# Packing the expert tables of a routed feed-forward layer into one word per entry

## The chip, the cores and the metric

The kernel runs on one core of a Trainium2 chip. The metric is the time of one execution on the device in microseconds. The time before is 2512.99 us, the median of three runs (2507.62 to 2515.87 us).

## The reference

One layer: linear attention with a residual, then a mixture of experts with a residual. The part that matters here is the second, over 4096 tokens of 512 numbers, with 32 experts, 8 of them for each token.

```python
E, K, H, F = 32, 8, 512, 192
scores = softmax(x @ wg.T)
weights, idx = top_k(scores, K)
weights = weights / sum(weights, axis=-1, keepdims=True)
order = argsort(idx.reshape(-1))                  # rows sorted by expert
xs = x[t_s]
g = ragged_dot(xs, w1, group_sizes)
u = ragged_dot(xs, v1, group_sizes)
ys = ragged_dot(silu(g) * u, w2, group_sizes)
out = zeros(T, H).at[t_s].add(ys * w_s[:, None])
...
x = x + layernorm(attention(layernorm(x)))
x = x + layernorm(moe(layernorm(x)))
```

How many rows an expert gets is known only at run time.

## The kernel before

The kernel has an attention part (to about 1165 us), a short stage that builds tables (to about 1211 us), the expert stage (to about 2440 us) and a final layer norm with the residual.

During the attention part every token's row is written eight times into a buffer in memory that is sorted by expert, in pages of 256 rows. In the table stage VectorE turns the page counts into tables in row 0 of the tile `bq`, as 32-bit integers:

- `table`, one column per expert: row 0 holds the expert's number of tiles `n`, row 1 the number of its `first` tile, row 2 the place of its padding rows (SyncE alone reads it), row 3 the value of the semaphore `s_D` (the count of `down` products) from which the expert before the last has left its weight slot. This block starts at L620 and ends with the signal `s_tabd` at L651. ScalarE, VectorE and SyncE wait for it.
- `at_tile`, one column per tile: row 0 holds the offset of the tile's weights in the tile `WB` (one of four slots, `WSET` = 4608 columns each), row 1 the first tile of its expert (GpSimd reads it), row 2 the place of its rows in memory (SyncE reads it). Column `g + 2` belongs to tile `g`. This block (L679 to L683) follows two small matrix products and ends with the signal `s_tiles`, for which SyncE, TensorE and GpSimd wait. Between the two blocks a list of pages is brought from memory (L356), and TensorE sums comparisons with it (L425).

In the expert stage a tile is 128 sorted rows of one expert. There are 276 tiles. Each number is split into a high part (float32r) and the rest, so that every product is made as three. For a tile TensorE does, in this order, `rows_t` of the tile after (four transposes, L437), `up` (12 matmuls of 384 columns, L446 to L448), `act_t` of the tile before (two transposes, L456) and `down` of the tile two before (five matmuls of 512 columns, L463 to L467). The loop over tiles is a hardware loop with four tiles per turn (L479). At the start of each tile TensorE's sequencer reads two words with `slot_at` (L470): the weight offset of the tile two before, for `down`, and that of the tile itself, for `up`.

ScalarE does for each tile `silu` (L513), the high part of the transposed activations (L518), the copy of `down`'s result to one of four buffers in `Y` (L524) and the high part of the transposed rows (L508). VectorE does the gate (L712, L715), the low part of the activations (L722), the tile's index for the add (L727) and the low part of the rows (L702, L704). GpSimd adds the result to the sum in memory with an indirect DMA (L1449). Waits are for semaphores, whose value is mostly computed from the tile's number in a register.

ScalarE and VectorE go by experts: `each_expert` (L291) reads `n` (L299) and `first` (L300) for an expert, then calls `convert`, then runs a hardware loop over the expert's `n` tiles (L565 on ScalarE, L754 on VectorE). `convert` splits the weights of the expert two ahead into one of the four slots, in six pieces: ScalarE writes the high part (L503), VectorE the low one (L601). ScalarE's `convert` reads a third word (L545), waits until `s_D` has reached it (L546) and issues, between its pieces, the transfers of the weights of the expert three ahead (L319 to L324). VectorE's `convert` reads nothing more. For the last two experts there is nothing to convert.

Of the kernel before, what the change touches and what calls it, by code (L numbers as in the profile page):

```python
# [7 lines left out]
EXPERTS, TOP_K, FFN = 32, 8, 192  # L8
P = 128
TOKENS = BATCH * SEQ  # L10
# [19 lines left out]
WSET = 2 * W13 + 3 * HID  # L30
WSETS = 4
# [13 lines left out]
def layer(nc, x_in, wkv_in, bq_in, bkv_in, wq_in, wo_in, wg_in, w13_in, w2_in, out):  # L45
# [9 lines left out]
    with ctx:  # L55
# [104 lines left out]
        tn = bq[:, 0:ES].rearrange("p (i n) -> p i n", i=4)  # L160
        step = bq[:, ES:ES + 2 * EXPERTS].rearrange("p (i n) -> p i n", i=2)
        table = bq[0:1, 2 * ES:2 * ES + 4 * EXPERTS].bitcast(i32).rearrange("p (i n) -> p i n", i=4)
        pair_n = bq[0:1, 3 * ES:3 * ES + 1].bitcast(i32)
        listed = bq[:, 3 * ES + 2:3 * ES + 2 + 2 * TILES // 4].rearrange("p (k j) -> p k j", j=2)
        at_listed = bq[:, 3 * ES + 32:3 * ES + 32 + TILES // 4]
# [128 lines left out]
        def each_expert(eng, convert, body):  # L294

            eng.wait_ge(s_tabd, 1)

            def one(e, q):
                n = eng.value_load(table[0:1, 0, bass.ds(e, 1)], min_val=1, max_val=TOKENS // P + 1)  # L299
                first = eng.value_load(table[0:1, 1, bass.ds(e, 1)], min_val=0, max_val=MAX_TILES)  # L300
                convert(e, q)
                body(e, q, first, n)
                return first + n

            with eng.Fori(0, EXPERTS // WSETS - 1) as r:
                for q in range(WSETS):
                    one(r * WSETS + q, q)
            for e in range(EXPERTS - WSETS, EXPERTS):
                total = one(e, e % WSETS)
            return total  # L310
# [102 lines left out]
        def moe_pe(pe):  # L413

            pe.sem_inc(s_T, RSLOTS)
            pe.sem_inc(s_U, 1)
            pe.sem_inc(s_H, 1)
            pe.sem_inc(s_D, 1)

            steps = TILES // 4  # L420
            pe.wait_ge(s_pld, 64)
            for k in range(steps + 1):
                pe.wait_ge(s_pcmp, k + 1)
                pages_of = listed[:, k, 1:2] if k < steps else col[:, 3:4]
                nc.tensor.matmul(bank[5][0:1, 0:MAX_TILES], pages_of, same[k % COMPARES], start=k == 0, stop=k == steps).then_inc(s_pmm, 1)  # L425

            pe.wait_ge(s_cmp, 1)
            for i in range(2):
                last = nc.tensor.matmul(bank[6 + i][0:1, 0:MAX_TILES], col[:, i:i + 1], iota_g[:, :], start=True, stop=True)
            last.then_inc(s_tmm, 1)  # L430

            def rows_t(g, i, p):
                s = i % 2
                pe.wait_ge(s_ld[i], 16 * p + 16)
                pe.wait_ge(s_exl, g)
                for k in range(KC):
                    last = nc.tensor.transpose(et[s][:, k * P:(k + 1) * P], xr[:, i, k * P:(k + 1) * P], ident[:, :])  # L437
                last.then_inc(s_T, 1)

            def up(g, s, off):  # L440
                pe.wait_ge(s_exl, g + 2)
                pe.wait_ge(s_h, g + 1)
                for k in range(KC):
                    wh = WB[:, bass.ds(off + k * UP, UP)]
                    wl = WB[:, bass.ds(off + (W13 + k * UP), UP)]
                    nc.tensor.matmul(eu[s][:, 0:UP], XL[:, s, k, :], wh, start=k == 0, stop=False)  # L446
                    nc.tensor.matmul(eu[s][:, 0:UP], XH[:, s, k, :], wh, start=False, stop=False)  # L447
                    last = nc.tensor.matmul(eu[s][:, 0:UP], XH[:, s, k, :], wl, start=False, stop=k == KC - 1)  # L448
                last.then_inc(s_U, 1)

            def act_t(g, s):

                pe.wait_ge(s_h, g + 3)
                pe.wait_ge(s_hl, g + 2)
                for c in range(2):
                    last = nc.tensor.transpose(eh[s][:, c * P:(c + 1) * P], hx[:, s, c * P:(c + 1) * P], ident[:, :])  # L456
                last.then_inc(s_H, 1)

            def down(g, s, off):
                pe.wait_ge(s_hl, g + 4)  # L460
                pe.wait_ge(s_y, g + 3)
                w2h, w2l, w2x = [WB[:, bass.ds(off + o, HID)] for o in (W2H, W2L, W2X)]
                nc.tensor.matmul(ed[s], SL[:, s, 0, :], w2h, start=True, stop=False)  # L463
                nc.tensor.matmul(ed[s], SH[:, s, 0, :], w2h, start=False, stop=False)  # L464
                nc.tensor.matmul(ed[s], SH[:, s, 0, :], w2l, start=False, stop=False)  # L465
                nc.tensor.matmul(ed[s], SL[:, s, 1, :], w2x, start=False, stop=False)  # L466
                nc.tensor.matmul(ed[s], SH[:, s, 1, :], w2x, start=False, stop=True).then_inc(s_D, 1)  # L467

            def slot_at(i):
                return pe.value_load(at_tile[0:1, 0, bass.ds(i, 1)], min_val=0, max_val=(WSETS - 1) * WSET)  # L470

            pe.wait_ge(s_ld[0], 16)
            for k in range(KC):
                last = nc.tensor.transpose(et[0][:, k * P:(k + 1) * P], xr[:, 0, k * P:(k + 1) * P], ident[:, :])
            last.then_inc(s_T, 1)
            pe.wait_ge(s_tiles, 1)
            pairs = pe.value_load(pair_n[0:1, 0:1], min_val=TOKENS * TOP_K // P // 2, max_val=PAGES // 2)

            with pe.Fori(0, pairs >> 1) as p:  # L479
                for i in range(RSLOTS):  # L480
                    g, s = RSLOTS * p + i, i % 2
                    before, now = slot_at(g), slot_at(g + 2)
                    rows_t(g + 1, (i + 1) % RSLOTS, p + (i + 1) // RSLOTS)
                    up(g, s, now)
                    act_t(g - 1, 1 - s)
                    down(g - 2, s, before)

            total = 2 * pairs
            rows_t(total + 1, 1, pairs >> 1)
            act_t(total - 1, 1)  # L490
            down(total - 2, 0, slot_at(total))
            down(total - 1, 1, slot_at(total + 1))

        def moe_act(act):

# [42 lines left out]
            act.wait_ge(s_T, RSLOTS + 2)  # L538
            nc.scalar.activation(XHF[:, HID:2 * HID], PS[:, ET + HID:ET + 2 * HID], ACT.Copy).then_inc(s_exh, 1)

            def convert(e, q):
                if isinstance(e, int) and e + 2 >= EXPERTS:
                    return
                load = not (isinstance(e, int) and e + 3 >= EXPERTS)
                before = act.value_load(table[0:1, 3, bass.ds(e, 1)], min_val=1, max_val=MAX_TILES + 3)  # L545
                act.wait_ge(s_D, before)  # L546
                stand(act)
                if load:
                    act.wait_ge(s_elo, e + 2)
                    stand(act)  # L550
                for piece in range(len(PIECES)):
                    weights_high(e + 2, (q + 2) % WSETS, q % 2, piece)
                    if load and piece < 4:
                        load_weights(act, e + 3, (q + 1) % 2, piece)
# [31 lines left out]
        def moe_dve(dve):  # L586
# [23 lines left out]
            def done(inst):  # L610
                tab[0] += 1
                inst.then_inc(s_tab, 1)

            def settled():
                dve.wait_ge(s_tab, tab[0])
# [20 lines left out]
            done(nc.vector.scalar_tensor_tensor(odd[:, 1:2], odd[:, 0:1], float(YSLOTS), total, ALU.mult, ALU.subtract))  # L636
            done(nc.vector.tensor_copy(step[:, 1, 1:EXPERTS], tn[:, 2, 0:EXPERTS - 1]))
            done(nc.vector.memset(step[:, 1, 0:1], 0.0))
            done(nc.vector.memset(step[:, 0, :], float(WSET)))
            settled()  # L640
            done(nc.vector.tensor_tensor(tn[:, 3, :], tn[:, 3, :], tn[:, 2, :], ALU.subtract))
            done(nc.vector.memset(step[:, 0, :].rearrange("p (r q) -> p r q", q=WSETS)[:, :, 0:1], float((1 - WSETS) * WSET)))
            done(nc.vector.tensor_scalar(odd[:, 2:3], odd[:, 0:1], float(YSLOTS // 2), None, ALU.mult))
            settled()
            done(nc.vector.memset(step[:, 0, 0:1], 0.0))
            done(nc.vector.tensor_tensor(tn[:, 2, EXPERTS - 1:EXPERTS], tn[:, 2, EXPERTS - 1:EXPERTS], odd[:, 1:2], ALU.add))
            settled()
            nc.vector.tensor_copy(table[:, 0:2, :], tn[0:1, 2:4, :])
            nc.vector.memset(table[:, 3, 0:1], 1)
            nc.vector.tensor_scalar(table[:, 3, 1:EXPERTS], tn[0:1, 3, 0:EXPERTS - 1], 3.0, None, ALU.add)  # L650
            nc.vector.tensor_copy(pair_n[:, :], odd[0:1, 2:3]).then_inc(s_tabd, 1)  # L651
            for i, (which, src) in enumerate(((ident[:, 0:EXPERTS], step[:, 0, :]), (ident[:, 0:EXPERTS], step[:, 1, :]), (fours, tn[:, 3, :]),
                                              (ident[:, 0:EXPERTS], iota_e[:, :]))):
# [22 lines left out]
            dve.wait_ge(s_pcmp, steps + 1)  # L676
            nc.vector.tensor_scalar(iota_g[:, :], iota_g[:, :], col[:, 2:3], None, ALU.is_ge).then_inc(s_cmp, 1)
            dve.wait_ge(s_tmm, 1)
            nc.vector.memset(at_tile[:, :, 0:2], 0)  # L679
            for i in range(2):  # L680
                nc.vector.tensor_copy(at_tile[:, i, 2:2 + MAX_TILES], bank[6 + i][0:1, 0:MAX_TILES])
            dve.wait_ge(s_pmm, steps + 1)
            nc.vector.tensor_scalar(at_tile[:, 2, 2:2 + MAX_TILES], bank[5][0:1, 0:MAX_TILES], float(PAGE), None, ALU.mult).then_inc(s_tiles, 1)  # L683

# [51 lines left out]
                nc.vector.tensor_tensor(XLF[:, half], PS[:, ET + i * HID:ET + (i + 1) * HID], XHF[:, half].bitcast(f32),  # L736
                                        ALU.subtract).then_inc(s_exl, 1)

            def convert(e, q):
                if isinstance(e, int) and e + 2 >= EXPERTS:  # L740
                    return
                for piece in range(len(PIECES)):
                    weights_low(e + 2, (q + 2) % WSETS, q % 2, piece)
# [836 lines left out]
```

## Time and profile before

| | |
|---|---|
| median of 3 runs | 2512.99 us |
| profiled execution | 2513.74 us |
| its span, first to last instruction | 2512.0 us |
| busy in the span: TensorE, VectorE, ScalarE, GpSimd | 90%, 59%, 49%, 38% |
| mean granted clock of TensorE | 0.955 of full |
| memory traffic over the span | 142 GB/s |

The table is from the profile's page and the list of runs. Busy time of an engine is time in which one of its instructions ran; register instructions and table loads of a sequencer are not counted in it. They have rows of their own, in which the engine's name ends in q (ACTq, DVEq, PEldq). A matmul's end is modelled, so two that follow each other overlap in the rows, and the distance of their starts is what TensorE takes for one. "issue" as the reason of a wait means that no signal of another engine is seen that ended it.

### The profile page before, as it was taken

Reading aid. Unit: us, or ns where it says so; the run is one execution under the profiler, and the core shown is the slowest. Engines: PE = TensorE matmul, PEld = TensorE weight load, DVE = VectorE, ACT = ScalarE, POOL = GpSimd, SP = SyncE. Lnnn points to the kernel's source line nnn. Section 1 sums busy time; section 2 is a strip of 40 time slices with the busy share of each in tenths; the row PEclk is TensorE's granted clock in tenths of the full one; section 3 lists DMA queues with packets and bytes.
Section 4 is the critical chain, followed back from the end, with each engine's and each line's share of the span. In section 5 each row is a group of like instructions: output and inputs, shape, how many; then the busy total and the mean of one; then the engine's idle time right before and its main releaser. Section 6 shows DMA issues by size and latency. Waiting matters only on the chain.

```text
span 2512.0 us, 63405 instructions
## 1 busy us (share of the span) xinstructions
PE 2250.3 (90%) x11850; PEld 1921.8 (77%) x11851; DVE 1488.6 (59%) x4833; ACT 1235.1 (49%) x2643; POOL 952.3 (38%) x1128
## 2 busy tenths in 40 slices
PE   7999899999989999991798999989999889989980
PEld 5887588888858888881597888868889778978970
DVE  4455567777767777773545555555554555455446
ACT  3344466656656665651344444454444444444433
POOL 1212025555535555556133333323333233323332
PEclk9999999999999999995899999999999999999995
DMA  3234103333342333325798888877777787777767
GB/s 118 89 116 121 59 26 115 120 114 128 122 134 103 123 119 114 128 102 196 200 204 179 179 190 185 170 178 164 151 150 140 169 162 156 140 168 142 139 111 288
DMA packets 165278, 358.64 MB, mean 143 GB/s; under 512 B 21216, under 2 KB 21216, under 8 KB 165088
## 3 DMA queue, kind: packets, MB, share of 16 engines
q0 software_dynamic: 60512, 144.74, 29.3%
q1 hardware_dynamic: 91264, 173.89, 23.3%
q10 hardware_dynamic: 13440, 39.33, 4.7%
q8 instruction: 22, 0.36, 0.1%
q14 instruction: 40, 0.33, 0.0%
HBM read 178.21 MB, written 179.66 MB: 142 GB/s over the span
## 4 chain that ended last, share of the span: by engine, by line
PE 37%; issue 5%; ACTq 4%; DMA 2%; ACT 2%; DVE 1%; DVEq 1%; POOL 1%; SPq 0%; POOLq 0%
PE bank L446 6%; PE bank L448 6%; PE bank L447 6%; PE bank L437 5%; PE bank L463 3%; PE bank L456 2%; PE bank L467 2%; PE bank L465 2%; PE bank L466 2%; PE bank L464 2%; ACTq L324 1%; ACT WB L503 1%; DVEq L712 1%; ACT BIG L582 1%; DMA moe_sum<-Y,aidx 1%
## 5 line engine op out<-in xcount | busy, mean ns | idle before, releaser
L1449 POOL DMA_INDIRECT moe_sum<-Y,aidx x276 | 428.6, 1553 | 835.5 <-issue 480.9
L929 PE MATMUL bank<-WB,XH 128*128 128x512 f32 x1536 | 477.1, 392 | 0.0
L446 PE MATMUL bank<-WB,XL 128*128 x1104 | 401.3, 363 | 0.0
L448 PE MATMUL bank<-WB,XH 128*128 x1104 | 375.7, 340 | 0.0
L447 PE MATMUL bank<-WB,XH 128*128 x1104 | 374.5, 339 | 0.0
L929 PEld LDWEIGHTS bank<-WB,XH 128*128 128x128 f32 x1536 | 290.4, 189 | 58.1 <-issue 0.5
L929 PE MATMUL bank<-WB,XL 128*128 128x512 f32 x768 | 315.5, 411 | 10.4 <-DVE XL L1236 10.4
L929 PE MATMUL bank<-WB,SH 128*128 128x512 f32 x1024 | 317.2, 391 | 0.0
L712 DVE SCALAR_TENSOR_TENSOR BIG<-BIG,bank x276 | 95.9, 347 | 363.1 <-ACT BIG L513 211.2
L1515 POOL DMA_INDIRECT sorted_rows<-BIG,pos x256 | 265.6, 1038 | 95.3 <-issue 95.3
L513 ACT ACTIVATE BIG<-bank x276 | 91.4, 331 | 354.5 <-PE bank L448 338.8
L524 ACT ACTIVATE Y<-bank x278 | 166.5, 599 | 180.7 <-PE bank L467 144.8
L1199 ACT ACTIVATE BIG<-BIG,rec 128x128 f32<-128x128 f32 x512 | 163.6, 390 | 181.2 <-DVE rec L1308 170.1
L929 PEld LDWEIGHTS bank<-WB,SH 128*128 128x128 f32 x1024 | 192.7, 188 | 37.6
L929 PE MATMUL bank<-WB,SL 128*128 128x512 f32 x512 | 211.0, 412 | 2.8 <-DVE WB L1298 2.8
L446 PEld LDWEIGHTS bank<-WB,XL 128*128 128x128 f32 x1104 | 213.1, 193 | 0.0
L447 PEld LDWEIGHTS bank<-WB,XH 128*128 128x128 f32 x1104 | 213.0, 193 | 0.0
L448 PEld LDWEIGHTS bank<-WB,XH 128*128 128x128 f32 x1104 | 210.8, 191 | 0.0
L1457 POOL TENSOR_SCALAR ve<-mv 128x1 f32<-128x1 f32 x128 | 47.0, 367 | 424.8 <-DVE mv L1227 302.1
L704 DVE TENSOR_TENSOR XL<-bank,XH x276 | 190.9, 692 | 18.0 <-ACT XH L508 3.8
L437 PEld LDWEIGHTS bank<-ident,BIG 128*128 128x128 f32 x1108 | 136.0, 145 | 76.2 <-issue 50.5
L437 PE MATMUL bank<-ident,BIG 128*128 128x128 f32 x1108 | 177.2, 284 | 16.4 <-issue 14.2
(211 smaller groups left out, 4265.2 us busy)
## 6 DMA issues: line engine op xcount, KB each, us to landing
BIG<-sorted_rows SPq DMA_DIRECT2D x278, 274.0 KB
Y<-x_in SPq DMA_DIRECT2D x64, 256.0 KB, 2.8
RAW<-w_in ACTq DMA_DIRECT2D x15, 768.0 KB
LATE<-w_in ACTq DMA_DIRECT2D x15, 768.0 KB
sorted_rows<-BIG SPq DMA_DIRECT2D x33, 274.0 KB, 12.3
moe_sum<-LATE SPq DMA_DIRECT2D x34, 256.0 KB, 3.0
LATE<-x_in SPq DMA_DIRECT2D x32, 256.0 KB
RAW<-wo_in SPq DMA_DIRECT2D x16, 512.0 KB, 3.5
```

The source lines that it names most:

```text
L437: last = nc.tensor.transpose(et[s][:, k * P:(k + 1) * P], xr[:, i, k * P:(k + 1) * P], ident[:, :])
L446: nc.tensor.matmul(eu[s][:, 0:UP], XL[:, s, k, :], wh, start=k == 0, stop=False)
L447: nc.tensor.matmul(eu[s][:, 0:UP], XH[:, s, k, :], wh, start=False, stop=False)
L448: last = nc.tensor.matmul(eu[s][:, 0:UP], XH[:, s, k, :], wl, start=False, stop=k == KC - 1)
L513: nc.scalar.activation(BIG[:, at(SG, parity, FFN, FFN)], PS[:, at(EU, parity, HID, FFN)], ACT.Silu).then_inc(s_sg, 1)
L524: nc.scalar.activation(YF[:, bass.ds(((g + YSLOTS) & (YSLOTS - 1)) * HID, HID)], PS[:, at(ED, parity, HID, HID)], ACT.Copy).then_inc(s_y, 1)
L704: nc.vector.tensor_tensor(XLF[:, at(0, parity, HID, HID)], PS[:, at(ET, parity, HID, HID)], XHF[:, at(0, parity, HID, HID)].bitcast(f32), ...
L712: nc.vector.scalar_tensor_tensor(BIG[:, at(HX, parity, 2 * P, P)], BIG[:, at(SG, parity, FFN, P)], w, PS[:, at(EU + FFN, parity, HID, P)], ...
L929: last = nc.tensor.matmul(ps, w, m, start=start and i == 0, stop=stop and i == len(terms) - 1)
L1199: last = nc.scalar.activation(sqn[:, c % 2, h * P:(h + 1) * P], e[:, c % 2, h * P:(h + 1) * P], ACT.Copy, scale=rec[:, c % 2, h:h + 1])
L1449: nc.gpsimd.indirect_dma_start(acc_dram[:, :], bass.IndirectOffsetOnAxis(aidx[:, s:s + 1], 0), rows, None, compute_op=ALU.add).then_inc(s_ ...
L1515: nc.gpsimd.indirect_dma_start(sorted_dram[:, :], bass.IndirectOffsetOnAxis(pos[:, s, k:k + 1], 0), srow[:, s, :], None).then_inc(s_sc[s], 16)
```

## The change

The tables are packed and the readers unpack them in registers.

- Each column of `table` row 0 becomes one word, `before * 32768 + n * 512 + first`. It is built in float32 from two partial sums and written as an integer. ScalarE and VectorE read it once per expert, in place of three and two words.
- The slots of the tiles are no longer summed up as offsets of `WB` but as numbers of experts (the step from one expert to the next is 1), and column `g` of `at_tile` row 0 becomes the expert of tile `g` plus 64 times the expert of tile `g - 2`. TensorE reads it once per tile, takes each slot with a mask of two bits and multiplies it by `WSET`.
- VectorE's two table blocks get the instructions for this. GpSimd's and SyncE's reads stay.

```diff
+        words = bq[0:1, 7 * ES - EXPERTS:7 * ES]
...
             def one(e, q):
-                n = eng.value_load(table[0:1, 0, bass.ds(e, 1)], min_val=1, max_val=TOKENS // P + 1)
-                first = eng.value_load(table[0:1, 1, bass.ds(e, 1)], min_val=0, max_val=MAX_TILES)
-                convert(e, q)
+                word = eng.value_load(table[0:1, 0, bass.ds(e, 1)], min_val=512 + 32768, max_val=512 * 32768 - 1)
+                first, n, before = word & 511, (word >> 9) & 63, word >> 15
+                convert(e, q, before)
...
-            def slot_at(i):
-                return pe.value_load(at_tile[0:1, 0, bass.ds(i, 1)], min_val=0, max_val=(WSETS - 1) * WSET)
+            def slots_at(i):
+
+                word = pe.value_load(at_tile[0:1, 0, bass.ds(i, 1)], min_val=0, max_val=64 * EXPERTS - 1)
+                return (word & (WSETS - 1)) * WSET, ((word >> 6) & (WSETS - 1)) * WSET
...
-                    before, now = slot_at(g), slot_at(g + 2)
+                    now, before = slots_at(g)
...
-            def convert(e, q):
+            def convert(e, q, before):
...
-                before = act.value_load(table[0:1, 3, bass.ds(e, 1)], min_val=1, max_val=MAX_TILES + 3)
                 act.wait_ge(s_D, before)
...
-            done(nc.vector.memset(step[:, 0, :], float(WSET)))
+            done(nc.vector.memset(step[:, 0, :], 1.0))
...
-            done(nc.vector.memset(step[:, 0, :].rearrange("p (r q) -> p r q", q=WSETS)[:, :, 0:1], float((1 - WSETS) * WSET)))
...
-            nc.vector.tensor_copy(table[:, 0:2, :], tn[0:1, 2:4, :])
-            nc.vector.memset(table[:, 3, 0:1], 1)
-            nc.vector.tensor_scalar(table[:, 3, 1:EXPERTS], tn[0:1, 3, 0:EXPERTS - 1], 3.0, None, ALU.add)
+            done(nc.vector.scalar_tensor_tensor(tn[0:1, 0, :], tn[0:1, 2, :], 512.0, tn[0:1, 3, :], ALU.mult, ALU.add))
+            done(nc.vector.memset(words[:, 0:1], 32768.0))
+            done(nc.vector.tensor_scalar(words[:, 1:EXPERTS], tn[0:1, 3, 0:EXPERTS - 1], 3.0, 32768.0, ALU.add, ALU.mult))
+            settled()
+            nc.vector.tensor_tensor(table[:, 0, :], words, tn[0:1, 0, :], ALU.add)
...
-            nc.vector.memset(at_tile[:, :, 0:2], 0)
-            for i in range(2):
-                nc.vector.tensor_copy(at_tile[:, i, 2:2 + MAX_TILES], bank[6 + i][0:1, 0:MAX_TILES])
+            nc.vector.memset(at_tile[:, 1:3, 0:2], 0)
+            nc.vector.tensor_copy(at_tile[:, 1, 2:2 + MAX_TILES], bank[7][0:1, 0:MAX_TILES])
+            done(nc.vector.tensor_copy(iota_g[0:1, :], bank[6][0:1, 0:MAX_TILES]))
+            settled()
+            nc.vector.tensor_copy(at_tile[:, 0, 0:2], iota_g[0:1, 0:2])
+            nc.vector.scalar_tensor_tensor(at_tile[:, 0, 2:MAX_TILES], iota_g[0:1, 0:MAX_TILES - 2], 64.0, iota_g[0:1, 2:MAX_TILES], ALU.mult, ALU.add)
+            nc.vector.tensor_scalar(at_tile[:, 0, MAX_TILES:MAX_TILES + 2], iota_g[0:1, MAX_TILES - 2:MAX_TILES], 64.0, None, ALU.mult)
```

## Rows read from the trace of the kernel before

**Rows 1.** Stretches: length, busy us of each engine, granted clock, DMA share, GB/s.
```profile
1213.00:2440.00 1227.00, 1139.63 (x6359) 1016.08 (x6359) 646.15 (x1842) 573.61 (x1286) 425.22 (x274) 0.97 0.80 165
```

**Rows 2.** Timeline of TensorE: start, length, line, operation, idle before.
```profile
1705.50 0.61 PE L437 MATMUL bank<-ident,BIG 128*128 128x128 f32 x4
...
1709.20 0.40 PE L467 MATMUL bank<-WB,SH 128*128 x1
1709.43 0.60 PE L437 MATMUL bank<-ident,BIG 128*128 128x128 f32 x4
...
1719.76 0.39 PE L467 MATMUL bank<-WB,SH 128*128 x1
1720.61 0.63 PE L437 MATMUL bank<-ident,BIG 128*128 128x128 f32 x4 [0.47 <-issue]
```

**Rows 3.** Waits, 1213 to 2440: who, for what, us in total, times, longest.
```profile
POOL moe_sum L1449 <- issue: 480.9, 189, 45.4
...
PE bank L456 <- DVE BIG L715: 69.4, 31, 3.4
...
ACT Y L524 <- POOLq L815: 16.9, 21, 1.5
...
PE bank L437 <- issue: 14.2, 32, 1.0
...
ACT WB L503 <- PE bank L467: 9.3, 3, 3.5
...
ACT WB L503 <- DMA RAW<-w_in: 6.5, 2, 3.4
ACT WB L503 <- DMA LATE<-w_in: 6.3, 2, 3.3
```

**Rows 4.** The chain of waits, 1710 to 1722: start, length, what.
```profile
1711.45 0.05 ACTq L300
...
1712.06 0.05 ACTq L545
...
1712.70 0.07 issue
...
1716.54 0.04 DVEq L754
...
1717.08 0.05 DVEq L712
1717.17 0.04 DVEq L712
...
1717.58 0.12 DVE BIG L712
```

**Rows 5.** Lines L545, L549, L300: ns min/median/max, first and last start.
```profile
L545 ACTq TENSOR_LOAD <-bq x30: 273/275/897, 1217.0 to 2275.2; - x30
...
L549 ACTq ALU_OP  x7: 35/35/42, 1217.7 to 2089.8; - x7
...
L300 DVEq TENSOR_LOAD <-bq x32: 300/306/777, 1217.2 to 2345.0; - x32
```

**Rows 6.** Line L470, whole and 1718.9 to 1720.5; L463, 1700 to 1704.
```profile
L470 PEldq TENSOR_LOAD <-bq x554: 295/301/1036, 1212.1 to 2438.9; - x185
...
L470 PEldq TENSOR_LOAD <-bq x2: 299/301/303, 1719.0 to 1719.8; - x2
...
L463 PEldq FUSED_REGOPS  x1: 46/46/46, 1702.9 to 1702.9; - x1
```

**Rows 7.** Timeline of VectorE.
```profile
1702.45 0.42 DVE L722 TENSOR_TENSOR SL<-bank,SH  x1
```

**Rows 8.** The chain of waits, 1180 to 1212.
```profile
1184.50 12.64 DMA bq<-page_list
```

**Rows 9.** Timeline of VectorE in the second table block.
```profile
1205.73 0.44 DVE L681 CAST bq<-bank 1x290 int32<-1x290 f32 x1 [1.32 <-issue]
...
1206.46 0.44 DVE L683 TENSOR_SCALAR bq<-bank 1x290 int32<-1x290 f32 x1
```

More of the change, by code:

```diff
@@ L490, in moe_pe @@
             act_t(total - 1, 1)
-            down(total - 2, 0, slot_at(total))
-            down(total - 1, 1, slot_at(total + 1))
+            down(total - 2, 0, slots_at(total)[1])
+            down(total - 1, 1, slots_at(total + 1)[1])
         def moe_act(act):
@@ L737, in moe_dve, with convert @@
                                         ALU.subtract).then_inc(s_exl, 1)
-            def convert(e, q):
+            def convert(e, q, before):
                 if isinstance(e, int) and e + 2 >= EXPERTS:
```

## Prediction

> **What bounds the kernel now.** I read three views in this order. The view by stretches for the expert stage, 1213 to 2440 us [rows 1], shows TensorE busy for 1139.6 of 1227 us, against 646 for VectorE and 574 for ScalarE: TensorE is the bound, and what is to be won is the rest. 276 tiles pass in the stage (554 loads of a slot [rows 6], two a tile and two at the end). The timeline of TensorE [rows 2] gives the pace of an undisturbed tile: its first transpose (L437) starts at 1705.50 and that of the next at 1709.43, so 3.93 us. 276 x 3.93 = 1085 us of 1227, so some 142 us are lost in the stage. The list of waits [rows 3] says on what. The largest is L456, the transpose of the activations, waiting for VectorE's gate (L715): 69.4 us in 31 waits, 2.2 us each. There are 30 experts whose turn carries a weight conversion (the third load of ScalarE, x30 [rows 5]), so this is one stall per expert. The second is L437 waiting for "issue", 14.2 us in 32 waits: TensorE's own sequencer comes too late with the next tile. The modelled end of L467 hides part of each: L467 to L437 is 0.23 us where nothing is missing (1709.20 to 1709.43) and 0.85 after a stall (1719.76 to 1720.61), of which the view calls 0.47 idle [rows 2]. So 0.16 a time belongs on top: 14.2 + 32 x 0.16 = 19 us. Third, the granted clock is 0.97 over the stage [rows 1]; with levels of 1 and 0.5 that is 6% of the stage, 74 us, at 1.2 GHz, which costs at most 37 us. 69 + 19 + 37 is 125 of the 142; the rest is spread over short waits and the stage's two ends.
>
> **ScalarE: two of three loads go.** The chain of waits through one turn of expert [rows 4] shows the stall's making. After the last XH of the old expert ScalarE's sequencer reads three table entries before it can start the conversion: the second runs from 1711.45 to 1712.06, the third from 1712.06 to 1712.70. Those two are removed: 0.61 + 0.64 = 1.25 us. In their place come shifts and masks on the word. On ScalarE only the shift for the count of `s_D` stands ahead of the conversion; such a register instruction took 0.035 us [rows 5], with what lies around it 0.07. The masks for `first` and `n` are needed only by the tile loop, which is issued while the last conversion piece still runs. So the conversion starts 1.18 us earlier.
>
> **VectorE: one of two loads goes.** Its load takes 0.306 us [rows 5] and with its address and its check about 0.75. It stands beside ScalarE's loads, since VectorE cannot convert before ScalarE's first piece. VectorE's chain matters at the other end: from L754, the entry to the tile loop, at 1716.54, to the gate L712 at 1717.58 is 1.04 us of register instructions, 0.09 from one to the next (1717.08 to 1717.17) [rows 4]. If the two masks and the shift for `first` and `n` are worked out there, they add 0 to 0.27 us; I take 0.2. The turn then gains 1.18 - 0.2, about 1.0 us. That is less than the stall of 2.2, so it comes off fully.
>
> It does not come off at every turn. Seven times ScalarE's conversion waited, with the loads done, for something else: 3 times for TensorE's L467 (9.3 us) and 4 times for a weight transfer (6.5 and 6.3 us) [rows 3]. These are experts of few tiles, where the transfer was issued by the turn before. I count nothing for them and 0.15 us each for the masks, 1 us lost. So 23 x 1.0 - 1 = 22 us. Bounds: 0.7 to 1.25 us a turn, that is 15 to 29.
>
> A rule of the Trainium skill would price the load otherwise: "DMA: Bandwidth & Descriptors", section "Latency and other measured facts", puts the floor of a `tensor_load` at about 600 ns. By that two loads less would be 1.9 us a turn, 1.6 after the masks, and the term 36 us; the trace has 0.3 us for the load itself [rows 5, 6], and its number is used.
>
> **TensorE: one of two loads a tile goes.** After a stall the two loads start at 1719.0 and 1719.8 [rows 6], with address and check 0.75 us each, and L437 follows. Without a stall they matter less, but do matter: down's wait is for a register's value, so the sequencer stands at it until VectorE's L722 ends at 1702.87 [rows 7], and issues L463's first register instruction at 1702.9 [rows 6]; down, the loop's branch and two loads then take it to 1705.3, when the array has just run dry. One load less is 0.75. The new mask, shift, mask and two multiplications are at most five register instructions of 0.09 (0.45), at least nothing where they fold into those that are there; I take 0.3, so 0.45 net. 32 waits x 0.45 = 14 us, and 3 for those too short to be listed: 17. Bounds: 5 (all five instructions in the way, and the short waits stay) and 24 (nearly all of the lost time).
>
> **The clock.** At a turn the array now stands for 2.2 us, then 0.6 again; afterwards 1.2 and about 0.1. Whether the grant falls less often the trace of before can't show. It is bounded by 0 and 37 us; the idle time halves, but the grant fell at some turns only, so I take a quarter, 9. A worse phase could also cost some: -5 at the low end.
>
> **What is added.** In the first table block VectorE has one dependent step more, some 0.3 us, covered by the page list's transfer, which is the chain itself from 1184.5 to 1197.1 [rows 8] while the block runs beside it. Without that cover it would cost those 0.3 us. In the second block three conversions of 1 x 290 follow each other from 1205.73 to 1206.90 [rows 9], and SyncE, TensorE and GpSimd wait for the last. Added behind them: the wait for a result, two operations of a few elements (0.1 each) and one of 1 x 290, 0.3 to 0.44: +0.6 us, all on the path. No DMA, queue or wait on a semaphore between engines is added.
>
> **What comes nearer.** The adds into `moe_sum` run on GpSimd's queue. ScalarE waited 21 times, 16.9 us, until one freed a buffer [rows 3]. With turns shorter this grows in the stretches with short experts. GpSimd itself waited 480.9 us for work [rows 3], so the adds can't bound the stage. I take 3 us.
>
> **Sum.** 22 + 17 + 9 - 0.6 - 3 = 44 us. The profiled execution took 2513.74 us (span 2512.0), 0.75 above the median of the runs; 2513.7 - 44 = 2469.
>
> **Rivals.**
> (A) TensorE's part is nothing: the masks and multiplications cost what the load cost, and the clock stays. For it: the sequencer runs ahead of the array for most of a tile. Against it: the 32 waits. Then 22 - 4 = 18 us: 2495. The Trainium skill speaks for (A): "Advanced Engine Details and Errata", section "Engine Queue Depths", gives TensorE a queue of 64, which would hide any load behind more than a tile's matmuls. By rows 6 and 7 the queue doesn't fill, because the wait for a register's value holds the sequencer itself.
> (B) The clock gives back most: 30 of 37 us instead of 9: 2449.
> (C) The turn is ended by something else than the loads, as it was 7 times: weights or adds come no earlier, and ScalarE waits at the conversion instead. Only TensorE's 17 less 3 are left, or with (A) nothing: 2500 to 2513, middle 2506. Against it: in the other turns the conversion started 0.2 us after the last load.
> (D) Slower: the masks are not kept but worked out again at each use. TensorE's `up` and `down` form an address in 11 register instructions a tile; with two more each of 0.09, the sequencer needs 2 us more a tile. It has 3.93 us for a tile and reaches the next transposes just in time now; less the 0.75 saved it would be late by 0.3 us or more from the point where the added instructions exceed the load removed. 276 x 0.3 = 83 us, less the turns' 22: 2575. Against it: a slot read before is used in the same 11 instructions with no repeated work.
>
> **How the numbers follow.** Forecast 0.52, (A) 0.20, (B) 0.13, (C) 0.10, (D) 0.05. A measurement of this kernel can tell 0.3%, 7.5 us, from no change. Faster by more: forecast, (A), (B) and half of (C), 0.90; within: half of (C), 0.05; slower: (D), 0.05. The forecast's own range, from the terms' bounds, is 2448 to 2490. The range takes in (A) and nearly all of (B) and leaves out (D) and most of (C): 2444 to 2498.
>
> **What would show it.** Right: L456's wait for L715 falls from 69 to about 45 us with as many waits; L437's wait for "issue" falls below 3; ScalarE shows one load a turn with the conversion's first piece some 1.2 us nearer to the last XH; the granted clock of the stage is 0.975 or more; `s_tiles`' last conversion ends 0.6 us later than now after the last table matmul. Wrong: as many masks in TensorE's register instructions as matmuls (D); waits of L503 on transfers in many more than 4 turns (C); L437's "issue" unchanged (A). The forecast fails as a whole if the stall at a turn isn't shortened by what ScalarE's loads gave up.

## The result, and the profile after

The kernel after takes 2478.39 us (median of 4 runs, 2474.85 to 2481.75) against 2513.86 for the kernel before beside it (2507.62 to 2515.87): ratio 0.9863, 95% interval 0.9841 to 0.9885. A later set of runs gave 2481.98 against 2515.14, ratio 0.9862 (0.9841 to 0.9884). By these the change saves 33 to 35 us, where 44 were forecast. The profiled execution of after took 2481.75 us (span 2479.9), 32 us less than the profiled one of before.

The list of waits of the kernel after over the expert stage, 1213 to 2440 us, as in [rows 3]: who waits, for what, us in total, times, longest. L457 is the old L456, L438 the old L437, L464 the old L463, L506 the old L503, L722 the old L715.
```profile
PE bank L457 <- DVE BIG L722: 63.5, 31, 5.7
...
ACT WB L506 <- DMA LATE<-w_in: 21.3, 5, 5.9
...
ACT Y L527 <- POOLq L822: 11.3, 15, 2.2
...
ACT WB L506 <- DMA RAW<-w_in: 9.2, 2, 5.5
...
PE bank L464 <- issue: 7.6, 26, 1.1
...
PE bank L438 <- issue: 1.1, 4, 0.3
```
A second profiled execution of this kernel (2479.12 us) has for the first of these rows:
```profile
PE bank L457 <- DVE BIG L722: 57.1, 30, 6.0
```
Against [rows 3] the reader is to see four things. The next tile's transposes are no longer late: 14.2 us in 32 waits have become 1.1 in 4. A wait that is nearly all new, 7.6 us in 26 (0.9 in 1 before), stands one step earlier, ahead of down's first matmul. The stall at an expert's turn fell by only 6 us, from 69.4 to 63.5, in the second execution by 12, and its longest grew from 3.4 to 5.7 and 6.0. And ScalarE's conversion waits 30.5 us in 7 places for a weight transfer (27.3 in 7 in the second execution), where it was 12.8 us in 4.

From the start of the first transposes inside the loop over tiles to the start of those behind it, in TensorE's timeline, the 276 tiles take 1190.1 us, against 1222.4 before (1184.9 in the second execution). So the 32 us between the profiled executions all lie in this stage.

An ordinary turn in TensorE's timeline (start, length, line, operation, idle before), first of the kernel before, then the same turn in the kernel after:
```profile
1718.24 0.44 PE L456 MATMUL bank<-ident,BIG 128*128 128x128 f32 x2 [2.19 <-DVE BIG L715]
```
```profile
1699.80 0.44 PE L457 MATMUL bank<-ident,BIG 128*128 128x128 f32 x2 [1.52 <-DVE BIG L722]
1700.49 0.49 PE L464 MATMUL bank<-WB,SL 128*128 x1 [0.26 <-issue]
...
1701.52 0.40 PE L468 MATMUL bank<-WB,SH 128*128 x1
1701.76 0.61 PE L438 MATMUL bank<-ident,BIG 128*128 128x128 f32 x4
```
The stall is 0.67 shorter. L468 to L438 is 0.24 us, the undisturbed distance, where it was 0.85 with 0.47 called idle [rows 2]. In its place 0.26 us of idle stand ahead of L464.

At the same turn ScalarE's timeline shows the conversion after its loads:
```profile
1712.92 0.53 ACT L503 ACTIVATE WB<-RAW 128x384 fp32r<-128x384 f32 x1 [1.97 <-issue]
```
```profile
1694.18 0.53 ACT L506 ACTIVATE WB<-RAW 128x384 fp32r<-128x384 f32 x1 [1.01 <-issue]
```
Counted over that timeline, the time from the end of the last XH of an expert to the start of the conversion has a median of 2.06 us before and 0.92 after (0.78 in the second execution), over 29 turns.

Two turns that follow each other closely, in the kernel before and in the kernel after (TensorE's timeline, then of after also ScalarE's and the chain):
```profile
1348.08 0.44 PE L456 MATMUL bank<-ident,BIG 128*128 128x128 f32 x2 [2.51 <-DVE BIG L715]
...
1357.29 0.44 PE L456 MATMUL bank<-ident,BIG 128*128 128x128 f32 x2 [3.21 <-DVE BIG L715]
```
```profile
1343.40 0.44 PE L457 MATMUL bank<-ident,BIG 128*128 128x128 f32 x2 [0.93 <-DVE BIG L722]
...
1353.02 0.69 PE L457 MATMUL bank<-ident,BIG 128*128 128x128 f32 x2 [4.91 <-DVE BIG L722]
```
```profile
1347.16 0.53 ACT L506 ACTIVATE WB<-LATE 128x384 fp32r<-128x384 f32 x1 [4.21 <-DMA LATE<-w_in]
```
```profile
1339.67 7.47 DMA LATE<-w_in
1347.16 0.06 ACT WB L506
```
The first stall fell from 2.51 to 0.93, the second rose from 3.21 to 4.91: 5.72 us together before, 5.84 after. The transfer for the second turn is issued by the first turn's conversions, and the second conversion starts as it lands. The distance of the two stalls' ends was 9.21 us and is 9.62. At this pair, what is saved at the first turn is waited for at the second.

Of the table part, the chain of waits of the kernel after, 1150 to 1222, still holds the transfer of the page list, as in [rows 8], so the longer first block is covered by it:
```profile
1184.00 13.74 DMA bq<-page_list
```
VectorE's timeline of the second block answers to [rows 9]:
```profile
1206.13 0.44 DVE L683 CAST bq<-bank 1x290 int32<-1x290 f32 x1 [1.32 <-issue]
...
1206.50 0.44 DVE L684 COPY bq<-bank 1x290 f32<-1x290 f32 x1
1206.97 0.16 DVE L686 CAST bq<-bq 1x2 int32<-1x2 f32 x1
1207.04 0.44 DVE L687 SCALAR_TENSOR_TENSOR bq<-bq 1x288 int32<-1x288 f32 x1
...
1207.48 0.44 DVE L690 TENSOR_SCALAR bq<-bank 1x290 int32<-1x290 f32 x1
```
From the start of the block's first conversion to the end of its last it is 1.79 us (1206.13 to 1207.92), where it was 1.17 (1205.73 to 1206.90): the added work is 0.6 us.

### The profile page after: what moved, and what is told of

Its sections match the earlier page's. It is cut to its first block, busy times and chain, and to the rows that moved or that the text cites. A ratio compares the mean times of both kernels' runs of the same rounds, so it can differ in the third digit from the quotient of the medians.

```text
span 2479.9 us, 64600 instructions
## 1 busy us (share of the span) xinstructions
PE 2232.1 (90%) x11850; PEld 1921.0 (77%) x11851; DVE 1485.7 (60%) x4836; ACT 1233.3 (50%) x2643; POOL 951.7 (38%) x1128
## 4 chain that ended last, share of the span: by engine, by line
PE 38%; issue 5%; DMA 4%; ACTq 3%; ACT 2%; DVE 1%; DVEq 1%; SPq 0%; POOL 0%; POOLq 0%
PE bank L447 6%; PE bank L449 6%; PE bank L448 6%; PE bank L438 4%; PE bank L464 3%; PE bank L457 2%; PE bank L468 2%; PE bank L466 2%; PE bank L465 2%; PE bank L467 2%; DMA LATE<-w_in 2%; ACTq L325 1%; ACT WB L506 1%; DMA moe_sum<-Y,aidx 1%; ACT BIG L584 1%
## 5 line engine op out<-in xcount | busy, mean ns | idle before, releaser
L438 PEld LDWEIGHTS bank<-ident,BIG 128*128 128x128 f32 x1108 | 141.0, 144 | 44.3 <-issue 6.0
L438 PE MATMUL bank<-ident,BIG 128*128 128x128 f32 x1108 | 171.4, 278 | 2.8 <-DMA BIG<-sorted_rows 1.7
```

## The experiments

All are timed in five rounds against the kernel before, except the two with smaller transfers (three).

**1. Which part gives what.** The experts' word alone, on the kernel before:
```
+                word = eng.value_load(table[0:1, 0, bass.ds(e, 1)], ...)
+                first, n, before = word & 511, (word >> 9) & 63, word >> 15
```


> The experts' word alone: ScalarE and VectorE read one word, TensorE still reads two. Theory (the saved loads come off at the isolated turns, but where the next turn waits for its weight transfer the gain ends in that wait): ScalarE's loads fall from 64 to about 22 us in the 30 turns, the wait between loads and conversion rises by 12 us or more, L456's stall falls by 10 to 20 us, the time by 12 to 20 us. Rival (the two parts don't interfere and the experts' part is the 22 us that were forecast, TensorE's the rest): 21 to 23 us faster. Rival (the experts' part gives nothing, all of the measured 35 us is TensorE's): within 5 us of before.

And TensorE's word alone:
```
+                word = pe.value_load(at_tile[0:1, 0, bass.ds(i, 1)], ...)
+                return (word & (WSETS - 1)) * WSET, ((word >> 6) & (WSETS - 1)) * WSET
...
-                    before, now = slot_at(g), slot_at(g + 2)
+                    now, before = slots_at(g)
```


> TensorE's word alone: one read a tile, ScalarE and VectorE as before. Theory: the wait of L437 for issue goes from 14.2 us to about 1, but in pairs of turns tied by a weight transfer what it gives is taken back by the wait for the transfer, and the masks ahead of down add 0.2 us a turn; 14 to 20 us faster. The sum of this and the experts' part alone is below or near the whole, 35 us. Rival (TensorE's part is the whole gain): 33 us or more faster. Rival (the masks cost what the load cost): within 5 us.

Measured: 2491.75 us, ratio 0.990 (0.9885 to 0.9915), and 2508.51, ratio 0.9967 (0.9953 to 0.9981), both against 2515.81. That is 24 us for the experts' word (above the 12 to 20 of the theory, close to the rival's 21 to 23) and 7 for TensorE's; together 31, and the whole change 33 to 35, so by their times the two nearly add up. TensorE's part alone is smaller than the term of 17, and below the 14 to 20 us that were expected of it. The waits of the kernel with TensorE's word alone, 1213 to 2410:
```profile
PE bank L457 <- DVE BIG L721: 73.2, 30, 4.4
...
PEld bank L438 <- issue: 6.2, 27, 0.5
PE bank L464 <- issue: 5.4, 21, 0.3
...
PE bank L438 <- issue: 0.2, 1, 0.2
```
L438's 14.2 us went, as forecast. But 5.4 came back at L464, and the turns' stall rose by 4, from 69.2 in the same stretch of the kernel before.

The times alone don't say where each part was won. For that, take the distance from the start of each matmul to the start of the next in TensorE's timeline over the 276 tiles, and sum up by how much each is above the median for its place. What is left, 1053 to 1057 us, is 276 tiles of medians. "Other" is all distances that are at none of the three places; it holds the time at the lower clock and the short waits, and can't be split further by these rows.

| kernel | ahead of `act_t` | ahead of the next transposes | ahead of `down` | other | 276 tiles, us |
|---|---|---|---|---|---|
| before | 74.5 | 25.5 | 8.8 | 60.5 | 1222.4 |
| experts' word alone | 59.3 | 29.4 | 8.4 | 49.8 | 1200.2 |
| TensorE's word alone | 78.2 | 4.6 | 14.3 | 63.6 | 1215.3 |
| after | 68.1 | 3.6 | 14.6 | 49.1 | 1190.1 |
| after, second execution | 61.6 | 4.1 | 14.3 | 50.8 | 1184.9 |
| after, one more load on ScalarE (experiment 4) | 76.5 | 4.8 | 14.9 | 58.7 | 1211.4 |
| after, one more load on TensorE (experiment 4) | 51.2 | 40.1 | 14.7 | 64.2 | 1223.2 |

TensorE's word takes some 16 us off its own two places, alone and with the experts' word. Alone it gets only 7 us faster, since the stall at the turns and the other distances rise by 4 and 3. The experts' word alone takes 15 us off the stall and 11 off the rest. The mean granted clock over whole executions goes the same way: 0.961 with the experts' word alone (6 executions) and 0.952 with TensorE's alone (10), beside 0.956 of the kernel before (21). With levels of 1 and 0.5 that is 28 us less and 18 us more at 1.2 GHz, worth at most 14 and 9 us.

**2. Does a weight transfer hold what the turns gain?** w1 and v1 of an expert are transferred to a quarter of their width from expert 3 on, on the kernel before and on the kernel after. These two kernels leave out three quarters of those weights and compute with older numbers in their place, so only their times are of use:
```
-                eng.dma_start(to[:, 0:W13], w13_in[bass.ds(e, 1), :, :]...)
+                cols = W13 if isinstance(e, int) and e < 3 else UP
+                eng.dma_start(to[:, 0:cols], w13_in[bass.ds(e, 1), :, 0:cols]...)
```


> The kernel before, with only a quarter of w1 and v1 brought from memory for experts 3 on (the rest of the buffer holds older numbers). By itself it is to be the base of the next run. Theory: the 7 turns that waited after their loads lose that wait (20 us minus 9), so 8 to 20 us faster than before. Rival (the waits are TensorE's or the adds', not the transfer's): under 4 us.

> The changed kernel with the same quarter of w1 and v1. Theory (the change's gain is cut by the weight transfers): it is 45 to 55 us faster than the kernel before with the same quarter, and the wait between loads and conversion is 9 to 12 us in all 30 turns in place of 39. Rival (the gain is cut by something else, GpSimd's adds or the masks): the distance between the two stays 32 to 38 us.

Measured: 2506.48 (ratio 0.9965, 0.9953 to 0.9977) and 2464.24 (0.9796, 0.9782 to 0.981). The shorter transfer gives 9 us where the loads are as they were and 14 where they are gone (2478.39 to 2464.24), and beside it the change is worth 42 us instead of 33 to 35, between the 45 to 55 of the theory and the 32 to 38 of its rival. So by the medians 7 to 9 us of the missing gain lay in transfers; with intervals of 3 to 6 us on each side the size is rough. In the kernel with both, ScalarE's waits for them fall from 30.5 to 15.9 us, and don't end:
```profile
PE bank L458 <- DVE BIG L723: 47.5, 30, 3.9
...
ACT WB L507 <- DMA LATE<-w_in: 9.2, 3, 3.4
...
ACT WB L507 <- DMA RAW<-w_in: 6.7, 2, 3.7
```

**3. The same from the waiting side.** On the kernel after, the transfer of w1 and v1 is signalled by itself; the first four pieces wait for it alone, and only the fifth for w2:
```
+        s_ew1, ew1_at = [s_bias, s_tz], [16, 16 * (SPARE // P)]
...
-                    act.wait_ge(s_ewr[i], (e - i) * 32 + 64)
+                    act.wait_ge(s_ew1[i], (e - i) * 8 + 16 + ew1_at[i])
+                if piece == 4:
+                    act.wait_ge(s_ewr[i], (e - i) * 24 + 48)
```


> The changed kernel, where a conversion's first piece waits only for its own part of the weights' transfer (w1 and v1), and its fifth piece for the rest (w2). Theory (at 7 or 8 turns the conversion waits for the last part of the transfer, 39 us in all turns of which some 30 above the 0.3 us of the others): 1 to 2 us less at each of these turns, 6 to 15 us faster than the changed kernel. Rival (the parts land together, or w1 and v1 land last, since all share the same DMA engines): within 3 us.

Measured: 2474.83, ratio 0.9837 (0.982 to 0.9855). ScalarE's waits for transfers are gone from the list, and the turns' stall is 10 us less than the 63.5 of after's first execution, 3 less than the 57.1 of its second:
```profile
PE bank L458 <- DVE BIG L725: 53.9, 31, 4.1
```
In the pair of turns above the second stall is 3.56 instead of 4.91 and the two are 8.28 us apart instead of 9.62. In the profiled execution the 276 tiles took 1180.9 us, 4 and 9 less than in the two of after. The median is only 3.6 lower than after's (6 to 15 were expected), and the intervals overlap. That transfers bind at close turns is shown by the rows; what freeing them is worth isn't settled.

**4. What one load costs ScalarE, VectorE and TensorE.** Each is the kernel after with one more load, its result unused. On ScalarE, once an expert, ahead of the wait for `s_D`:
```
+                spare = act.value_load(table[0:1, 2, bass.ds(e, 1)], ...)
                 act.wait_ge(s_D, before)
```


> The changed kernel with one read put back on ScalarE ahead of each conversion (its value isn't used). Theory (a load costs 0.61 us at each turn whose conversion follows its loads, nothing at the 7 or 8 turns that wait for a transfer, and the grant of the clock adds some): 12 to 20 us slower than the changed kernel. Rival (the stalls are set by something else, and the experts' word gave its time by VectorE's load or the clock): under 5 us slower.

On VectorE, once an expert, ahead of its conversions:
```
+                spare = dve.value_load(table[0:1, 2, bass.ds(e, 1)], ...)
                 for piece in range(len(PIECES)):
```


> The kernel after with one more table load on VectorE, unused, once an expert, ahead of its six weight conversions (VectorE again makes two loads a turn, about 0.75 us more). Theory: VectorE's conversions follow ScalarE's piece by piece, one piece takes 2.3 to 2.4 us and VectorE has slack in each, so its own load is hidden behind ScalarE's first piece: within 5 us of the kernel after (2474 to 2484, ratio 0.984 to 0.988), and the gain of the experts' word is nearly all ScalarE's. Rival (the prediction's wording, a turn of both engines): VectorE's load lies on the path as ScalarE's does, 0.75 us by 30 turns, about 15 to 22 us over the kernel after (2493 to 2500, ratio about 0.993).

On TensorE, once a tile:
```
                 word = pe.value_load(at_tile[0:1, 0, bass.ds(i, 1)], ...)
+                spare = pe.value_load(at_tile[0:1, 2, bass.ds(i, 1)], ...)
```


> The kernel after with one more table load on TensorE, unused, in each tile of the experts' stage (two loads a tile again, with the instructions of the word on top). Theory: what the one load fewer gives beside the experts' word is the difference of the kernel after to the kernel with the experts' word alone, about 13 us, and the added load costs 0.5 us more where TensorE's queue is short, so 12 to 22 us over the kernel after (2490 to 2500, ratio 0.989 to 0.994), with L438's waits for issue back at 14 us or more. Rival: the two parts add up as they do alone (7 us of 2516), so 5 to 9 us over the kernel after, 2483 to 2487, ratio about 0.988.

Measured, with the kernel after again beside the last two (2481.98):

| one more load on | us | ratio to before | over after |
|---|---|---|---|
| ScalarE, x30 | 2503.23 | 0.9949 (0.9931 to 0.9967) | 21 to 25 |
| VectorE, x30 | 2487.98 | 0.9893 (0.987 to 0.9915) | 6 |
| TensorE, x278 | 2515.08 | 0.9992 (0.998 to 1.0004) | 33 |

ScalarE's load costs 0.7 to 0.8 us a turn over the 30 turns, above the 12 to 20 us that were expected. Not all of it is the path of the load. The conversion starts 1.54 us after the last XH (median), where it was 0.92 and 0.78, so 0.6 to 0.8 us later. The stall rises from 63.5 and 57.1 to 71.8. The other distances (table of experiment 1) rise by 8 to 10 us, and the mean granted clock is 0.953 in six executions, beside 0.958. The load itself has a median of 0.277 us:
```profile
L548 ACTq TENSOR_LOAD <-bq x30: 272/277/775, 1219.1 to 2264.2; - x30
```
VectorE's costs 6 us by the medians, with intervals that overlap those of after. In its trace the turns' stall is 65.8 us, beside 63.5 and 57.1 in the two traces of after. The 0.993 that the rival gave lies above its interval (0.987 to 0.9915), and ScalarE's price, 21 to 25 us, further still: the gain of the experts' word is for the most part ScalarE's.

TensorE's load came out above both expectations. With it the kernel is no faster than the kernel before. The waits of that kernel, 1213 to 2410:
```profile
PEld bank L438 <- issue: 71.3, 123, 1.4
PE bank L457 <- DVE BIG L723: 45.8, 29, 5.3
...
PE bank L438 <- issue: 17.2, 38, 0.9
...
PE bank L464 <- issue: 7.0, 27, 0.3
```
The weight load of the transposes is late for "issue" in 123 tiles instead of 26. Two loads and the word's masks are more than TensorE's sequencer gets done in a tile: the median distance of two tiles, counted over TensorE's timeline, is 4.03 us instead of 3.93. Every fourth tile loses most, the last of the loop's turn, with a median of 0.50 us from L468 to L438 against 0.23 in the other three. In these rows it is 0.37 in one tile and 0.24 in the next:
```profile
1795.48 0.40 PE L468 MATMUL bank<-WB,SH 128*128 x1
1795.85 0.65 PE L438 MATMUL bank<-ident,BIG 128*128 128x128 f32 x4
...
1799.64 0.40 PE L468 MATMUL bank<-WB,SH 128*128 x1
1799.88 0.60 PE L438 MATMUL bank<-ident,BIG 128*128 128x128 f32 x4
```
At the same time the turns' stall is 45.8, not 57.1 to 63.5: a TensorE that comes late to a turn waits less there. So the two terms of the sum are tied, and whoever speeds TensorE up between turns can lose part of it at the turns.

**5. The register instructions of `down` and of the tile loop.** On the kernel after, the old slot is put into a register of its own before `up`:
```
+                    before = pe.snap(before)
```


> The changed kernel, with the slot for down worked out on TensorE's sequencer before up instead of after the stall. Theory (three register instructions stand between the end of the stall and down, 0.2 us a turn, and that is what TensorE's word costs): TensorE's L464 waits for issue fall from 7.6 to under 1.5 us, the stretch from act_t to down loses 5 to 6 us, the time falls by 4 to 7 us against the changed kernel (to about 2473 where that is 2478). Rival (the masks there are hidden, the missing gain went elsewhere): within 2 us of the changed kernel.

Measured: 2478.97, ratio 0.9847 (0.9829 to 0.9865), equal to after; the 4 to 7 us of the theory did not come. L464 still waits 7.8 us for "issue" in 28 times, so the 0.26 us stayed where they were. What stands behind the wait in the kernel after is three instructions a tile, where the kernel before had one [rows 6]; the profile of line L464, 1698 to 1706, two tiles:
```profile
L464 PEldq ALU_OP  x4: 36/36/36, 1700.2 to 1703.6; - x4
L464 PEldq FUSED_REGOPS  x2: 60/60/60, 1700.4 to 1703.7; - x2
```
In the snapped kernel they are the same in number and place. No run has these three ahead of the wait, so what they cost by themselves is not measured.

**6. All together.** The snap, VectorE's `first` and `n` put into registers after the fourth piece, and the split wait; once in the set of runs with the split wait, once beside the kernel after:


> The changed kernel with the two edits above (the slot for down ahead of up, the split wait) and a third: VectorE works out first and n between its fourth and fifth conversion piece in place of after the last. Theory: the edits add up, snap_pe's gain plus split_wait's plus 3 to 4 us for VectorE's 0.16 us a turn. 2455 to 2468. Rival (the turns are now bound by the adds and transfers): no faster than the better of the two.

> The kernel with the experts' word, the tile's word, both counts put into registers of their own earlier, and the first four pieces waiting only for the transfer of w1 and v1; again, beside the kernel after on one chip. Theory: it is 3 to 8 us under the kernel after of this call. Rival: on one chip the two are equal within 2 us, and the 5 us between their medians so far were between chips.

> The kernel after once more, so that the three above are compared on one chip: 2474 to 2483, ratio 0.984 to 0.988. If it is elsewhere by more than 4 us, the differences of a few us between runs of different calls (the kernel with TensorE's count snapped, the one with the split wait) say nothing.

Measured: 2473.14, ratio 0.9839 (0.9821 to 0.9856), then 2478.14, ratio 0.9834 (0.9812 to 0.9857), beside after's 2481.98, ratio 0.9862 (0.9841 to 0.9884). Side by side it is 4 us below after, and by ratios 0.002 to 0.003 in both sets. The intervals overlap each time: likely a little faster, not shown, and short of the 2455 to 2468 that were expected. It is not faster than the split wait alone (2474.83), so neither snap did anything that can be told.

## Why the prediction was right, and where a size was off

The direction, the stage and the mechanism hold: what ScalarE reads ahead of its work at a turn, and TensorE ahead of a tile, was on the path. 2478.4 lies inside 2444 to 2498, 9 us over the forecast. The term that was mis-sized is that of the turns: 22 us were summed up, and the stall gave 6 and 12 in two executions, since the turns tied to a transfer lost time instead of none and TensorE's gain was partly waited for there. One of the signs named for being right did not come: L456's wait was to fall to about 45 us and fell to 63.5 and 57.1. By the steps of the sum:

- **The turns' term, 22 us: too large, the mis-sized one.** The experts' word alone gave 24 us, but that agreement with 22 is luck: the stall fell by 15 (69.4 to 54.7), and 11 more came from the other distances, where the clock is. With both words the stall fell by 6 and 12 in two executions. That a turn gains about 1 us was nearly right where no transfer binds: 24 such turns summed to 51.6 us before, 30.9 with the experts' word alone, 33.2 and 29.1 in two executions of after, so 0.8 to 0.9 each. The conversion starts 1.14 us nearer to the last XH (medians), as forecast. The masks in VectorE's loop entry cost 0.16 us, where 0.2 was taken (from its last conversion to the gate, 0.34 instead of 0.18 in the timeline).
- **"I count nothing" for turns tied to a transfer: too kind.** They were not neutral. In the six that followed another turn closely, and one more that joined them, the stall rose from 17.8 to 23.6 us with the experts' word alone, and to 30.3 and 27.7 in two executions of after. There the end is set by the landing, and what comes earlier before it is waited for. That is most of why L457's wait fell to 63.5 or 57.1 and not to about 45.
- **VectorE's load beside ScalarE's: right**, by the kernel with one more load on it: some 6 us against ScalarE's 21 to 25.
- **TensorE's term, 17 us: right for its own waits, not for the time.** Its two places gave 16 us (34.3 to 18.2 in the table of experiment 1). L438's wait went as forecast (14.2 to 1.1). The masks were priced rightly too: 0.3 us was taken, and 7.6 us in 26 waits at L464 is 0.29 each. In time it measured 7 alone and 9 to 13 on top of the experts' word (2491.75 against 2478.39, ratios 0.990 against 0.9863). The step that failed is that what TensorE gains between turns comes off in full beside the turns' term. TensorE arrives earlier at the turns: the stall is 54.7 us with the experts' word alone and 57.1 and 63.5 with both, 2 to 9 us given back. Two executions of one kernel differ by 6 there, so the size is rough; the direction is borne out by the kernel with one more load on TensorE (45.8).
- **Rival (A), TensorE's part nothing: wrong**, by 7 us of 2516 with an interval clear of 1, and by the 33 us that a second load costs. But what it gave for the time, 2495, is near the 2491.75 of the experts' word alone. The Trainium skill's queue of 64 entries for TensorE ("Advanced Engine Details and Errata", section "Engine Queue Depths") would hide both loads, as the prediction estimated from it; no run here agrees with that for loads behind a wait on a register's value.
- **Rival (C), another end of the turn: its mechanism came true in 7 turns of 30**, and cost roughly the 7 to 9 us of experiment 2. It was taken as a case by itself; it is a share of the main one. That the conversion is always late for something else did not come true.
- **The clock, 9 us: borne out in size, though the quarter was a guess.** The mean granted clock over whole executions is 0.955 for the kernel before (17 executions beside the second set of after) and 0.958 for after (8), that is 226 and 208 us at 1.2 GHz and at most 9 us of time. It rose with the experts' word alone and fell with TensorE's alone and with one more load on ScalarE, so in these runs it went with the stall at the turns. One trace can't show this: summing the clock records over the 276 tiles, 78.5 us were at 1.2 GHz in before, 64.9 and 58.0 in two executions of after, but 41 and 71.7 in two executions of the kernel of experiment 6, whose tiles took 1176.6 and 1189.3.
- **The table block, 0.6 us: right.** **The adds' 3 us:** ScalarE's wait for them fell, 16.9 to 11.3; the term was nothing.
- **Rival (D), masks at each use:** they come once a tile, so it didn't happen. But its margin was real: with one load more the transposes' weight load is late in 123 tiles, for 33 us.

## What to carry to other kernels

A load taken off the path pays where the waiting engine's own sequencer ends the wait; go through the turns one by one and ask at each whether a transfer lands later, since a saving between two events tied by a transfer can be paid back in full. Terms of a sum that end at the same wait need not add up: price the faster engine's earlier arrival as more waiting there. A time that agrees with a term doesn't show that the term was right; split it by place first (of the 22 us between the profiled executions of before and of the experts' word alone, 15 were stall and 11 other distances, less 4 ahead of the next transposes). How near a sequencer is to its limit is worth measuring with one added load: here it cost 0.12 us a tile (33 us over 276), where taking one away gave 0.03 to 0.05.

## What the runs showed of the hardware

The table load takes the same 0.27 to 0.30 us at its least on all three engines (ScalarE 272 ns, VectorE 300, TensorE 295), but with one more load ScalarE's conversion starts 0.6 to 0.8 us later and the kernel takes 0.7 to 0.8 us a turn longer, some of it at the lower clock. The Trainium skill's floor of about 600 ns for a `tensor_load` ("DMA: Bandwidth & Descriptors", section "Latency and other measured facts") is not that of the bare instruction in this trace; it is near the load with its address and check, 0.61 us in [rows 4]. ScalarE's load is at times much longer, up to 1032 ns in the kernel after, and what makes it so stays open: in the timeline of the kernel after the long ones and nearly all the short ones alike start while an activation issued just ahead still runs.
```profile
L300 ACTq TENSOR_LOAD <-bq x32: 272/296/1032, 1216.2 to 2312.0; - x32
```
The same load costs 33 us on TensorE and 6 on VectorE, in one kernel.
